# Two sixteen-head attentions: score matmuls on row halves, masks split between them, other masking in the local one

## What is computed

```
L1_attn_a (causal): y = softmax(q k^T / sqrt(8) + slope[h] * key_position, keys <= query) v ; x += y Wo
    slope[h] = base ** (h+1), base = 2 ** (-8/16)   (the relative-position bias; a row's constant drops out)
L3_attn_b (local):  y = softmax(q k^T / sqrt(8), |key - query| <= 128) v ; x += y Wo + bo
```

## Time and profile before

| | us |
|---|---|
| three runs | 3564.14, 3575.45, 3583.17; median 3575.45 |
| the profiled execution | 3585.18, its span 3583.1 (2.1 around it) |
| PE busy in the span | 2880.5 (80%) |
| DVE, ACT, POOL busy | 1859.3, 1405.9, 765.2 |
| causal attention | 1195 to 1563: front to 1252, pipeline from there |
| local attention | 3189 to 3470: front to 3233, pipeline from there |

### The profile page before, as it was taken

One profiled execution on the slowest core, in us unless ns is written; L12 is line 12 of the kernel. 1 busy time (PEld: TensorE's weight loads), 2 busy tenths in 40 slices (PEclk: granted clock), 3 DMA queues, 4 the chain that ended last, 5 costly groups with the idle time before them and its releaser, 6 DMA issues. The chain is left out here.

```text
span 3583.1 us, 54951 instructions
## 1 busy us (share of the span) xinstructions
PE 2880.5 (80%) x21418; PEld 1480.1 (41%) x21486; DVE 1859.3 (52%) x3533; ACT 1405.9 (39%) x2681; POOL 765.2 (21%) x632
## 2 busy tenths in 40 slices
PE   6565878778888498989768888998888877768986
PEld 3454247423357234434322222342332434555555
DVE  5311245478964388711378888203763543536733
ACT  3211424432234246642356777422221222234652
POOL 1000006245617201000443340003530001230003
PEclk9666869878889789989879999997998989878987
DMA  2022001121101422100031010000510001023302
GB/s 109 15 63 74 0 12 45 37 72 65 53 20 51 112 44 37 21 1 0 14 70 28 12 24 1 0 0 17 145 49 0 0 1 48 20 71 62 51 6 70
DMA packets 86479, 136.40 MB, mean 38 GB/s; under 512 B 13319, under 2 KB 52199, under 8 KB 84947
## 3 DMA queue, kind: packets, MB, share of 16 engines
q1 hardware_dynamic: 79187, 118.50, 13.1%
q0 software_dynamic: 7040, 14.43, 1.5%
HBM read 106.81 MB, written 25.85 MB: 37 GB/s over the span
## 5 line engine op out<-in xcount | busy, mean ns | idle before, releaser
L1655 ACT ACTIVATE at_pt<-PS 128x384 f32<-128x384 f32 (+3 forms) x704 | 288.5, 455 | 237.7 <-PE PS L1567 202.5
L1705 DVE TENSOR_REDUCE at_mp<-PS 128x1 f32<-128x384 f32 (+3 forms) x640 | 313.5, 538 | 115.1 <-PE PS L1555 98.9
L1552 PE MATMUL PS<-at_kx,at_qx 72*128 72x384 bf16 (+5 forms) x640 | 219.0, 347 | 66.8 <-DMA at_kx<-L_attn_a_parts 26.8
L1565 PE MATMUL PS<-at_qx,at_kx 105*128 105x512 bf16 (+5 forms) x704 | 214.4, 314 | 7.8 <-ACT at_pt L1655 5.9
L4300 DVE CUSTOM_DVE_ANT_0 PS<-PS,ls_pt 128x1024 f32<-128x1024 f32 x128 | 153.8, 1237 | 19.1 <-ACT ls_pt L4153 15.5
L4153 ACT ACTIVATE ls_pt<-PS,ls_far 128x512 f32<-128x512 f32 x256 | 155.5, 686 | 18.6 <-PE PS L3974 10.1
L2425 DVE TENSOR_TENSOR_SCAN mb_ring<-PS,mb_ring 128x1024 f32<-128x1024 f32 x64 | 146.6, 2291 | 19.4 <-POOL mb_ring L2364 6.7
L2380 PE MATMUL PS<-mb_ring,ident 128*128 128x512 f32 x256 | 147.2, 728 | 6.0 <-DVE mb_ring L2430 6.0
L1227 DVE SCALAR_TENSOR_TENSOR X<-PS,small_L,X 128x512 f32<-128x512 f32 x8 | 6.0, 751 | 261.2 <-PE PS L1175 261.2
L2409 ACT ACTIVATE PS<-mb_dt,mb_a 128x1024 f32<-128x1024 f32 x64 | 71.5, 1118 | 174.8 <-DVE mb_ring L2425 169.5
L1578 PE MATMUL PS<-at_pt,at_v 128*9 128x256 f32 (+3 forms) x1408 | 130.7, 451 | 5.5 <-issue 1.4
(11 more groups left out here) (825 smaller groups left out, 6557.2 us busy)
## 6 DMA issues: line engine op xcount, KB each, us to landing
rw_arena<-rw_v_rows SPq DMA_DIRECT2D x32, 512.0 KB, 4.6
dl_arena<-in_fir_bank SPq DMA_DIRECT2D x32, 256.0 KB, 3.1
lnA<-mb_rows SPq DMA_DIRECT2D x16, 512.0 KB, 3.7
XN<-mb_rows SPq DMA_DIRECT2D x16, 512.0 KB, 3.7
ffn_place<-in_ffn_L SPq DMA_DIRECT2D x4, 1152.0 KB, 16.7
at_qx<-L_attn_a_parts SPq DMA_DIRECT2D x24, 192.0 KB
at_kx<-L_attn_a_parts SPq DMA_DIRECT2D x72, 64.0 KB
at_qx<-L_attn_b_parts SPq DMA_DIRECT2D x24, 192.0 KB
```

The lines of the kernel that those rows point to most:

```text
L1552: mm = nc.tensor.matmul(PS[:, n % 3, 0:e - c], QX[0:RAW, u % 3, g, blk(i, P)], KX[0:RAW, u % 3, g, c:e], start=True, stop=True)
L1565: mm = nc.tensor.matmul(PS[:, 3 + n % 3, 0:e - c], KX[0:FULL, u % 3, g, blk(j, P)], QX[0:FULL, u % 3, g, c:e], start=True, stop=True)
L1655: nc.scalar.activation(PT[:, y % SLOTS, g, 0:e - c], PS[:, 3 + n % 3, 0:e - c], ACT.Exp, scale=SCALE).then_inc(exp_done, 1)
L1705: nc.vector.tensor_reduce(best, sc, AX.X, ALU.max).then_inc(s_maxed, 1)
```

## The change

The 128 rows of the two tiles become two lanes of 64, and two of a unit's four heads lie in each. Of the nine products of parts six are kept (`SPLIT`), so that a score contracts over 48 rows, in the causal kernel 54 (six rows of slopes; three more rows for the maxima in the second pass). A score and the transposed score issued beside it are always in different lanes. A mask is now two matmuls over the 64 rows of the score's own lane, 128 and 64 columns wide, and the masks of both are issued after both scores. In the local kernel the second pass has no masks on PE: POOL sets the masked exponentials in `PT` to zero, 1 or 2 operations of 128 by 4 by 128 values for each step (14 a unit), and `values` waits for them. The slopes are made bf16 on POOL during the layernorm and come in by DMA with each load, the positions' rows by six DMAs after piece 0, and the first load is issued after piece 3 instead of 4. Both long memsets of unused rows (L1392, L1394) go. A load has 18 DMAs (22 causal), each half's maxima two.

```diff
+    masks_first = lambda x: [j for j in range(first[x][1] // P, first[x][2] // P) if (j == first[x][0] if causal else j != first[x][0])]
+    cut_count = lambda u, x: u * sum(len(c) for c in cuts) + sum(len(c) for c in cuts[:x])
+    masks_second = cuts if causal else [[] for _ in second]
...
+    LANES, SPLIT = 2, ((0, 0), (0, 1), (0, 2), (1, 0), (1, 1), (2, 0))
+    SLOPES = 6 if causal else 0
+    PLACE = 8 * len(SPLIT)
+    RAW = PLACE + SLOPES
+    FULL = RAW + 3
+    EACH = HG // LANES
+    LOADS = LANES * (9 + (EACH if causal else 0))
+    lane_rows = lambda lane, n: slice(64 * lane, 64 * lane + n)
+    head_first = lambda t: 2 * (t % 2) + t // 2
+    head_second = lambda t: 2 * (1 - t % 2) + t // 2
...
-        QX, KX = sb("at_qx", [P, 3, HG, SEQ], BF16), sb("at_kx", [P, 3, HG, SEQ], BF16)
+        QX, KX = sb("at_qx", [P, 3, HG // LANES, SEQ], BF16), sb("at_kx", [P, 3, HG // LANES, SEQ], BF16)
...
+            tokens = blk(u // 4, SEQ)
+            for lane in range(LANES):
+                heads = slice(HG * (u % 4) + EACH * lane, HG * (u % 4) + EACH * lane + EACH)
+                top = 64 * lane
+                for p, (c, _) in enumerate(SPLIT):
+                    sp.dma_start(QX[top + 8 * p:top + 8 * p + 8, u % 3, :, :], parts[0, heads, c, :, tokens].rearrange("g d t -> d g t")).then_inc(LOADED[u % 3], 16)
+                for at, n in ((0, 3), (24, 2), (40, 1)):
+                    sp.dma_start(KX[top + at:top + at + 8 * n, u % 3, :, :], parts[1, heads, 0:n, :, tokens].rearrange("g c d t -> (c d) g t")).then_inc(LOADED[u % 3], 16)
+                if causal:
+                    for g in range(EACH):
+                        slopes = SLT[0:SLOPES, heads.start + g, :].unsqueeze(1).to_broadcast([SLOPES, 8, SEQ // 8])
+                        sp.dma_start(QX[top + PLACE:top + RAW, u % 3, g, :].rearrange("p (r t) -> p r t", r=8), slopes).then_inc(LOADED[u % 3], 16)
...
+                own(pool.tensor_copy(EYE2[:, 0:64], k.identb[:, 64:P]))
+                own(pool.tensor_copy(EYE2[:, 64:P], k.identb[:, 0:64]))
+                for n in range(2):
+                    sign = 2 * n - 1
+                    own(pool.memset(OTHER[:, n, :], 0.0))
+                    own(pool.memset(TURN[:, :], 0.0))
+                    own(pool.affine_select(out=OTHER[:, n, :], in_=OTHER[:, n, :], compare_op=ALU.is_ge, fill=NEG, base=-64 * sign, pattern=[[sign, P]], channel_multiplier=-sign))
+                    own(pool.affine_select(out=TURN[:, :], in_=TURN[:, :], compare_op=ALU.is_ge, fill=NEG, base=64 * sign, pattern=[[sign, P]], channel_multiplier=-sign))
+                    own(pool.tensor_copy(OTHER[64:P, n, :], TURN[64:P, :]))
...
-                    own(pool.memset(QX[64:96, :, :, :], 0.0))
-                else:
-                    own(pool.memset(KX[64:96, :, :, :], 1.0))
+                    for n in range(3):
+                        own(pool.tensor_tensor(RM[:, n:n + 1], k.ident[:, n:n + 1], k.ident[:, n + 3:n + 4], ALU.add))
+                    own(pool.tensor_copy(SH[:, 0, :], SL[:, :]))
+                    own(pool.tensor_tensor(SL[:, :], SL[:, :], SH[:, 0, :], ALU.subtract))
+                    own(pool.tensor_copy(SH[:, 1, :], SL[:, :]))
+                    own(pool.tensor_tensor(SH[:, 2, :], SL[:, :], SH[:, 1, :], ALU.subtract))
+                    for n in range(3):
+                        own(pool.tensor_scalar(SLR[:, n, :], SH[:, n, :], RM[:, n:n + 1], None, ALU.mult))
+                    own(pool.tensor_tensor(SLR[:, 0, :], SLR[:, 0, :], SLR[:, 1, :], ALU.add))
+                    own(pool.tensor_tensor(SLR[:, 0, :], SLR[:, 0, :], SLR[:, 2, :], ALU.add))
+                    own(pool.tensor_copy(SLT[0:SLOPES, :, :], SLR[0:SLOPES, 0, :].unsqueeze(2).to_broadcast([SLOPES, 16, SEQ // 8])))
+                own(pool.memset(UNIT[:, :], 1.0))
...
-                        if m == 4:
+                        if m == 0:
+                            for lane in range(LANES):
+                                for n, rows in enumerate(KROWS):
+                                    at = 64 * lane + PLACE + 3 * n
+                                    sp.dma_start(KX[at:at + 3, :, :, :].rearrange("p s g t -> p (s g) t"), rows[0:3, :].unsqueeze(1).to_broadcast([3, 3 * EACH, SEQ])).then_inc(PLACED, 16)
+                        if m == 3:
                             for n in range(4):
                                 sp.wait_ge(STORED[n], 48)
-                            if causal:
-                                sp.wait_ge(rows_made, 1)
-                                for slot in range(3):
-                                    sp.dma_start(KX[96:105, slot, :, :], KROWS[96:105, :].unsqueeze(1).to_broadcast([9, HG, SEQ])).then_inc(PLACED, 16)
                             load(sp, 0)
...
+                def mask(bank, at, kind, lane):
+                    rows = lane_rows(lane, 64)
+                    for half, eye, above in ((lane, k.identb, ABOVE), (1 - lane, EYE2, OTHER)):
+                        a, b = (64 * half, P) if kind == 0 else (0, 64 + 64 * half)
+                        mm = nc.tensor.matmul(PS[:, bank, at + a:at + b], eye[rows, :], above[rows, kind, a:b], start=False, stop=True, skip_group_check=True)
+                    return mm
...
+                    if cuts[x] and not causal:
+                        pe.wait_ge(cut_done, cut_count(u, x + 1))
...
+                            if p < UNITS and x < G1:
+                                score_masks(p, x, t)
+                            if 1 <= p <= UNITS and x < G2:
+                                turned_masks(p - 1, x, t)
...
+                def cut(u, x):
+                    h, j, c, e = second[x]
+                    pool.wait_ge(exp_done, N2 * u + HG * x + HG)
+                    for i in cuts[x]:
+                        sign = 1 if i <= j else -1
+                        v = PT[:, (G2 * u + x) % SLOTS, :, i * P - c:(i + 1) * P - c]
+                        pool.affine_select(out=v, in_=v, compare_op=ALU.is_ge, fill=0.0, base=0, pattern=[[0, HG], [sign, P]], channel_multiplier=-sign).then_inc(cut_done, 1)
...
-                    sp.dma_start(QX[MROW:MROW + 3, u % 3, :, blk(h)], lows[h]).then_inc(LOWERED[h], 16)
+                    for lane in range(LANES):
+                        sp.dma_start(QX[64 * lane + RAW:64 * lane + FULL, u % 3, :, blk(h)], lows[h][:, EACH * lane:EACH * lane + EACH, :]).then_inc(LOWERED[h], 16)
```

143 lines of the change are left out of this document (56 added, 87 removed).

## The result

Six runs of the changed kernel have a median of 3562.59 us (3554.22 to 3569.12), six of the kernel before 3575.19 (3564.14 to 3583.17): 12.6 us or 0.4% less, ratio 0.9958 with an interval of 0.9939 to 0.9978. Forecast were 3531 and a gain of 44.

The account below looks back on a forecast made before the run. PE was taken to set the local period, with PE and DVE close in the causal one. Causal -31.7 and local -12.5 gave -44 on 3585.2, 3541; with the median 9.7 lower, 3531 us, range 3500 to 3564.

Parts of the forecast that it names:

- lanes and masks: Causal periods: PE's work 25.4 us instead of 31.6, longest-engine step sum 31.1 instead of 33.5; -17 over seven periods.
- the casts: Causal pipeline: without POOL's cast the padding falls from 2.80 to .19 us six times, -13 (ends -13 and -23).
- (a): Local pipeline: POOL becomes a step's bound with cuts of 1.16 us, local +12 instead of -12.5, total 3556; chance 10%.
- (b): Local pipeline: DVE's small operations wait behind POOL's cuts, 3.8 us a period instead of .5, total 3554; chance 5%.
- The bounds of the two periods: Before, PE set the local period, PE and DVE were close in the causal; after, DVE longest: 27.4 causal, 18.85 local.
- The front: Causal front: SP's queue ends last, keys arrive sooner, PE starts at about 1249.3: -2.7 us (ends -8 and +3).
- local front: Before the local scores: memset gone saves 2.0 us, load issued one piece earlier 2.0, together -4 (ends 0 and -6).
- The local cuts: POOL's cuts in local second passes: .64 us each, mostly covered by scores, tail gap 4.9; -.75 a period, -5 over seven.
- DVE behind POOL: Local period: DVE held up beside POOL's cuts, as the padding was by the cast, .5 us a period.
- Rival (d): Both pipelines: granted clock falls to 1.2 GHz, low for .8 of a period, 79 us lost, total 3645; chance 6%.
- last periods: Second pass alone at each pipeline's end: causal -1 us by fewer mask waits, local -2.
- the maxima's second DMA: Causal pipeline: one more issue between split and transposed score, +.3 us a period, +2 in all (ends 0 and +5).

## Why the prediction was right or wrong

The way was right and the size wrong. Of the 36 us that are missing in the two stages, about 19 lie in the local periods and at the ends of both pipelines, where the clock was taken as 1.00 and was not, 10 in the two fronts, and 10 in the gain of lanes and masks in the causal periods; the casts give 3 back. That the time still fell into the range is luck: its upper end was there for rivals (a) and (b), and neither came.

**The bounds of the two periods** were read rightly. DVE came in PE's place in the causal period, which is 30.9 at full clock against a sum of step maxima of 31.1. What was wrong is the other side of that subtraction: I had 33.5 for a period before without casts, and the run without them has 32.5. A model that is off by 1 on a term of 2.4 gave 17 for the lanes and masks where the runs show 1.6 a period at equal clock, and 4.8 in six periods as they ran. The first row of the seven, 32.0 between two paddings, had said so. The mean of 35.4 that seemed to confirm 33.5 holds a projection in one period (37.1 for 32.5 in the run without casts) and three stretches at .50, and one cast fewer than I counted; that the sum met it was luck.

**The casts** gave 16 us by the run without and 19 by the run with them, for 13. The price of the wait was right, 2.2 each at equal clock; it came five times and not six (the sixth padding, at 1491.99, is .19 already), 11 us. The rest is the clock, which fell after three of them in the kernel before and which the sum left out. The upper end, 3.9, came from measured periods of unlike clock (36.4 at .95) and so held both. PE, as forecast, never waits for a DMA in the six periods: the slopes' and the maxima's cost nothing there.

**The front** was the first term with a wrong sign. -2.7 was forecast, +4.1 measured. The forecast named SP's queue as what ends last and then mispriced it: six position DMAs took 7.0 instead of 4.8 (.7 to 1.75 each), the load 9.9 instead of 8.6, the wait for the fourth piece's landing 1.9 instead of nothing. It also held that POOL's constants were covered; they end the layernorm in both kernels, 16.7 and 17.1 us after the stage's start, where its own work ends at 12, so they cost .5. In the local front -.5 for -4: the memset's going did give 2.1, as forecast (the projections start at 10.3 instead of 12.4), but from there to the first score it took 32.7 instead of 31.1, where -2.0 was forecast. There too the front ends with SP's last store, behind a load of 18 issues for 12 and two of positions (1.6 us).

**The local cuts** took 635 ns (.64 forecast), and the period's end gap at full clock 5.14 (4.9 forecast): the size was right. DVE behind POOL was priced at .5 and is less. In DVE's timeline, the copy of the splits, beside a cut and alone:

```profile
3389.22 0.42 DVE L1756 CAST at_mh<-at_mr 16x128 bf16<-16x128 f32 x1
...
3400.19 0.21 DVE L1756 CAST at_mh<-at_mr 16x128 bf16<-16x128 f32 x1
```

A cast, and not only the two-input padding, is held up, by .2 here and by .37 at most (580 ns against 214 for L1756), eight times of sixteen; that is under 2 us in the stage, so rival (b) is out by size. The rule of the Trainium skill (SBUF — State Buffer, Who interferes with whom) holds in this.

**The clock** is the step that failed most. Rival (d) had the mechanism, and was given 6% as one event, the whole pipeline at half clock. What came was a share of it: 17 us at .50 in the causal last period (none before), and 63 us in the local stage from the end of its first period to its own end (16 before). The forecast's sum took 1.00 for every period, and even its last periods as gains of 1 and 2; they lost 5.1 and 6.3. The causal 5.1 is that of one trace: in the run with the positions from POOL's queue these periods took 59.6 at .97, .4 more than before. The local loss came in every run with POOL's cuts. Local periods at full clock take 25.4 and 25.5 (the last of the six, and one in that same run) and would have been under before's 25.6 and 25.8. That it is the clock and not a mean over unlike periods is seen inside one trace: a period with the same work takes 27.7 at .81 and 25.4 at 1.00. That it fell because the change took work from PE is supported by the run with PE's masks (clock back, 11.4 us less), but why it falls is not shown: lanes used in turn instead of together had .50 through most of the local stage though PE was busier, 32-row zeros went with a lower clock in the local periods and 128-row ones with a higher, and neither the busy share of the records nor the rows of the scores explain all the runs.

**Sum.** The causal stage was forecast at -31.7 and came at -13.9. Of the 17.8 between, 6.8 are the front; 9.6 the lanes and masks in the six periods (-4.8 for -14.4), less 3.1 by the casts and 1.7 by the maxima's second DMA, which shows in no period; 8.2 the last two periods (+5.1 for -3.1); less 2.4 at the stage's end, where the clock was 1.00 in this trace and .64 before, which was not forecast. The rest is the first period and rounding. The local one was forecast at -12.5 and came at +5.9: 3.5 by the front, 1.4 by the first period, 2.8 by the six periods (-1.7 for -4.5), 9.0 by the last two (+6.3 for -2.7), 1.5 at the end.

## What to carry to other kernels

When work leaves the bounding engine, first build the period without the other term (here: the kernel before without its casts) and forecast against that, since a model's error is as large as the gain; and compare measured periods only at equal clock: a difference of whole periods holds what the clock did as well. Treat the matmul clock as a term of the sum wherever the change thins PE's work, above all in pipeline ends where a second pass runs without a first beside it, and not as an all-or-nothing rival. For a front, add up the issues of the queue that must be empty before a barrier, each at the price of its own shape, and look for an engine whose queue is idle in that stage.

## What the runs showed of the hardware

- Two matmuls over 54 and 57 rows in different halves of the rows start within .02 us; in the same half the next starts .12 us after one of 256 columns and .22 after one of 512. At full clock that is 2.4 us of a 31 us period.
- Between matmuls over 54 or 57 rows and ones over 128 rows .09 to .10 us are lost at each change, at a clock of 1.00.
- A POOL cast of 6 x 4096 elements (3.6 us) holds up a DVE operation with two SBUF inputs for 2.6 us, and a cut of 635 ns a DVE cast for up to .37. After three of five such holds in the kernel before, the clock stood at .50 for 3.4 us, at 1.6 us each; without the casts it did not.
- The granted clock stood at .50 through 38 us with PE busy 37.32 by its records, and through 52 with 52.00, and at 1.00 through 25 with 19.50. One and the same addition of matmuls in the local stage went with clocks of .92 to 1.00 when they contracted over 128 rows, and .50 to .86 over 32; in the causal last two periods they went with .97 and 1.00, and eight runs without them with .82 to .97. I have no rule that fits all of it.
- A DMA that writes 3 rows six times over cost SP .7 to 1.75 us to issue, and POOL .6 to .7.
